# A third place for turned rows, and two small subtractions moved ahead of a larger one, in an fp32-accurate attention and expert kernel

## What is computed

```python
q = (hidden_states @ Wq.T).reshape(B, L, H, D)
k = (hidden_states @ Wk.T).reshape(B, L, KVH, D)
v = (hidden_states @ Wv.T).reshape(B, L, KVH, D)
q = _apply_rope(q, cos, sin)          # the "turned" rows
k = _apply_rope(k, cos, sin)
dt = softplus(hidden_states @ Win.T + dt_bias); g = dt * -exp(A_log_bias)
G = cumsum(g) within a chunk of 128 tokens
scores  = q_chunk @ k_chunk.T ; decay = causal exp(G_i - G_j)
y_intra = (scores * decay) @ (v * dt)
cstates = (k * exp(Glast - G)).T @ (v * dt)      # state handed to the next chunk
y_inter = (q * exp(G)) @ previous state
y = rmsnorm(y_intra + y_inter) * gnorm_w * silu(hidden_states @ Wg.T)
out = y @ Wo.T
```

## Time and profile before

| what | value |
|---|---|
| time, median of 3 runs | 2247.51 us (2245.24 to 2248.74) |
| the profiled execution: its span | 2250.0 us |
| PE busy | 2100.6 us, 93% of the span |
| DVE busy | 1834.7 us, 82% |
| ACT busy | 1402.0 us, 62% |
| POOL busy | 1040.2 us, 46% |
| chain that ended last | 77% PE, 6% DVE, 6% issue, 4% POOL |

### The profile page before, as it was taken

One profiled execution on the slowest core, in us unless ns is written; L12 is line 12 of the kernel. 1 busy time (PEld: TensorE's weight loads), 2 busy tenths in 40 slices (PEclk: granted clock), 3 DMA queues, 4 the chain that ended last, 5 costly groups with the idle time before them and its releaser, 6 DMA issues.

```text
span 2250.0 us, 34037 instructions
## 1 busy us (share of the span) xinstructions
PE 2100.6 (93%) x9568; PEld 1630.9 (72%) x9568; DVE 1834.7 (82%) x3440; ACT 1402.0 (62%) x2732; POOL 1040.2 (46%) x828
## 2 busy tenths in 40 slices
PE   5899999999999999998999999999999999999993
PEld 3677777777777777776677777777777777767772
DVE  5888888888888888868888888888888888737886
ACT  5566666666666666653566666666666666626782
POOL 1344444445454544434364545454545454534661
PEclk8899999999999999999899999999999999979996
DMA  7212121212121212135121212121212121217668
GB/s 255 79 46 58 46 56 47 56 47 56 44 58 38 64 37 66 35 87 173 38 66 38 67 36 62 35 63 38 66 38 66 38 66 38 76 61 255 217 215 315
DMA packets 147547, 182.31 MB, mean 81 GB/s; under 512 B 12935, under 2 KB 89319, under 8 KB 147454
## 3 DMA queue, kind: packets, MB, share of 16 engines
q1 hardware_dynamic: 137310, 155.52, 24.3%
q0 software_dynamic: 8704, 25.21, 3.1%
q10 hardware_dynamic: 1440, 0.58, 0.1%
HBM read 152.90 MB, written 28.37 MB: 81 GB/s over the span
## 4 chain that ended last, share of the span: by engine, by line
PE 77%; DVE 6%; issue 6%; POOL 4%; ACT 3%; DMA 2%; SPq 1%; DVEq 0%; POOLq 0%; ACTq 0%
PE PJ L1242 11%; PE PJ L1244 10%; PE PJ L1243 10%; PE OU L1242 5%; PE OU L1244 5%; PE OU L1243 5%; PE TR L1392 5%; PE YE L1244 2%; PE YE L1243 2%; PE YE L1242 2%; PE SC L1242 2%; PE CS L1242 2%; PE YI L1242 2%; PE CS L1244 2%; PE CS L1243 2%
## 5 line engine op out<-in xcount | busy, mean ns | idle before, releaser
L457 POOL TENSOR_TENSOR zl<-yb,zh 128x512 fp32r<-128x512 f32 x122 | 162.9, 1335 | 318.9 <-ACT zh L972 318.8
L1242 PE MATMUL OU<-woh,zh 128*128 128x512 f32 x488 | 230.4, 472 | 17.7 <-POOL wol L708 10.2
L1765 DVE TENSOR_TENSOR t<-PJ,cosb 128x512 f32<-128x512 f32 x160 | 110.3, 689 | 156.6 <-PE PJ L1244 110.7
L1242 PE MATMUL PJ<-xnh,wqh 128*128 128x512 f32 x544 | 225.4, 414 | 7.9 <-DVE t L1767 7.4
L988 ACT ACTIVATE qh<-t 128x512 fp32r<-128x512 f32 x128 | 80.9, 632 | 218.6 <-DVE t L1770 218.6
L1243 PE MATMUL PJ<-xnl,wqh 128*128 128x512 f32 x544 | 213.9, 393 | 0.0
L1244 PE MATMUL PJ<-xnh,wql 128*128 128x512 f32 x544 | 213.6, 393 | 0.0
L1242 PE MATMUL PJ<-xnh,wgh 128*128 128x512 f32 x512 | 209.1, 408 | 2.9 <-POOL wgl L708 2.9
L1243 PE MATMUL PJ<-xnl,wgh 128*128 128x512 f32 x512 | 204.7, 400 | 0.0
L738 POOL TENSOR_TENSOR gm<-gbc,amask 128x512 f32<-128x512 f32 x128 | 166.9, 1304 | 81.6 <-DMA gbc<-decay_exponents 48.3
L1244 PE MATMUL PJ<-xnh,wgl 128*128 128x512 f32 x512 | 204.4, 399 | 0.0
(11 more groups left out here) (547 smaller groups left out, 6381.7 us busy)
## 6 DMA issues: line engine op xcount, KB each, us to landing
gbc<-decay_exponents SPq DMA_DIRECT2D x128, 256.0 KB, 4.9
stage<-in_wq SPq DMA_DIRECT2D x72, 256.0 KB
stage<-in_wg SPq DMA_DIRECT2D x64, 256.0 KB
stage<-in_wo SPq DMA_DIRECT2D x64, 256.0 KB
gbc<-in_wm SPq DMA_DIRECT2D x48, 256.0 KB
stage<-in_wkv SPq DMA_DIRECT2D x34, 256.0 KB
experts<-in_wm SPq DMA_DIRECT2D x16, 512.0 KB, 5.9
experts<-expert_rows SPq DMA_DIRECT2D x16, 512.0 KB, 13.9
```

The costliest lines, as they stand in the source:

```text
L457: nc.gpsimd.tensor_tensor(lo[:], yb[:, c, :], hi[:].bitcast(F32), ALU.subtract).then_inc(S["zlo"], 1)
L1242: nc.tensor.matmul(out_, a_hi, b_hi, start=first, stop=False)
```

## The change

The turned rows get a table of places, `rope_at`: tile 0 in the first half of `t2`, tile 1 in the second, tile 2 in `y2`, tile 3 in the first half, tile 4 in the second. The waits follow from it: tile 2 waits for the transposes of the raw values, tile 3 for the low part and the transposes of tile 0, tile 4 for the low part of tile 1 (before: of tile 2). On DVE the two subtractions `knlo` and `q3lo` stand ahead of `vw_lo(0)`, and `knlo` ahead of `q3lo`. No computing instruction is added or removed.

```diff
+        rope_at = [t2[:, 0, :], t2[:, 1, :], y2[:], t2[:, 0, :], t2[:, 1, :]]
...
                     def rope_lo(i, hi, lo):
                         at.wait("ropehi", i + 1)
-                        g.tensor_tensor(lo, t2[:, (5 * b + i) % 2, :], hi.bitcast(F32),
+                        g.tensor_tensor(lo, rope_at[i], hi.bitcast(F32),
...
-                            a.activation(hi, t2[:, (5 * b + i) % 2, :], ACT.Copy).then_inc(S["ropehi"], 1)
+                            a.activation(hi, rope_at[i], ACT.Copy).then_inc(S["ropehi"], 1)
...
                         def rope(i, bank):
 
-                            slot = (5 * b + i) % 2
+                            turned = rope_at[i]
                             at.wait("proj", (1, 3, 4, 5, 6)[i])
                             if i == 0:
                                 at.before("ropelo", 4)
                             elif i == 1:
                                 at.before("q3lo", 1)
+                            elif i == 2:
+                                at.wait("tr", 1)
+                            elif i == 3:
+                                at.wait("ropelo", 1)
+                                at.wait("tr", 2)
                             else:
-                                at.wait("ropelo", i - 1)
-                            if i == 2:
-                                at.wait("tr", 2)
+                                at.wait("ropelo", 2)
...
-                        vw_lo(0)
-
-                        at.wait("ropehi", 5)
-                        v.tensor_tensor(ql[:, 3, :], t2[:, (5 * b + 4) % 2, :], qh[:, 3, :].bitcast(F32),
-                                        ALU.subtract).then_inc(S["q3lo"], 1)
                         at.wait("knhi", 1)
                         v.tensor_tensor(knl[:], TR[:, 0:3 * P].rearrange("p (a b) -> p a b", a=3),
                                         knh[:].bitcast(F32), ALU.subtract).then_inc(S["knlo"], 1)
+                        at.wait("ropehi", 5)
+                        v.tensor_tensor(ql[:, 3, :], rope_at[4], qh[:, 3, :].bitcast(F32),
+                                        ALU.subtract).then_inc(S["q3lo"], 1)
+                        vw_lo(0)
```

More of the change, by code:

```diff
@@ L1419, in step @@
                         for i in range(3):
-                            ins = nc.tensor.transpose(TR[:, i * P:(i + 1) * P], t2[:, (5 * b) % 2, i * P:(i + 1) * P],
+                            ins = nc.tensor.transpose(TR[:, i * P:(i + 1) * P], rope_at[0][:, i * P:(i + 1) * P],
                                                       ident[:])
@@ L1765, in rope @@
                             v.tensor_tensor(t1[:], PJ[bank][:], cosb[:], ALU.mult)
-                            v.tensor_tensor(t2[0:hd, slot, :], PJ[bank][hd:D, :], sinb[0:hd, :], ALU.mult)
-                            v.tensor_tensor(t2[hd:D, slot, :], PJ[bank][0:hd, :], sinb[hd:D, :],
+                            v.tensor_tensor(turned[0:hd, :], PJ[bank][hd:D, :], sinb[0:hd, :], ALU.mult)
+                            v.tensor_tensor(turned[hd:D, :], PJ[bank][0:hd, :], sinb[hd:D, :],
                                             ALU.mult).then_inc(S["roperd"], 1)
                             at.wait("roperd", i + 1)
-                            v.tensor_tensor(t2[:, slot, :], t1[:], t2[:, slot, :], ALU.add).then_inc(S["rope"], 1)
+                            v.tensor_tensor(turned, t1[:], turned, ALU.add).then_inc(S["rope"], 1)
                         def weigh(c):
```

## The result

| | before | changed kernel |
|---|---|---|
| median of 6 runs each, us | 2245.15 (2236.71 to 2248.74) | **2226.81** (2212.69 to 2230.52) |
| ratio, 95% interval | | 0.9912 (0.9886 to 0.9939) |
| profiled execution, us | 2250.0 (span) | 2222.85, span 2221.1 |

What follows compares the result with a forecast made beforehand. PE was taken to bound the kernel, starting the scores late by at most 36.9 us in all. Gains of 0.88 us per step, 15 x (0.88 + 0.88) = 26.4, took the median from 2247.5 to 2221.5, range 2213 to 2236.

Steps and rivals of the forecast that it cites:

- The chain and the cause of the idle before the fifth tile: Fifth tile's sum, vwlo, q3lo, then scores; DVE idles 1.19 us before that tile, waiting for its place in `t2`.
- No effect: Rival: the idle before the fifth tile has another cause than the place, so time stays 2247.5; chance 0.05.
- The sum: DVE's sum of the fifth turned tile, b = 0: ends at 884.15 instead of 885.36, behind POOL's second `ql`.
- The held low part: DVE's `q3lo` before the scores, b = 0: behind POOL's `gm` it ends at 885.86, against 885.53 undisturbed.
- the middle of the three prices: `q3lo` with b = 0 ends at 885.53 undisturbed, 885.86 behind `gm`, or 886.05 behind a fully held `gm`; 885.86 taken.
- The new wait before `CS`: PE waits for DVE's `vwl` before the `chunk_state(0)` product, 0.2 to 0.4 us.
- The full hold of the shared data path: DVE's sum delays POOL's `gm` by its whole length; lower bound, gains 0.69 (b = 0) and 0.70 (b = 1), 20.9 us in all.
- PE's idle before the scores: PE's total wait before the scores' product falls from 31.9 to about 5 us, left only with b = 0.
- Each part alone gives little: Old place with new order leaves `chunk_state(0)` at 887.9 as now; the gain is the place's, the order lets it through.
- Given back at intra(0): Rival: `wfl` or pieces ahead meet POOL longer, PE loses up to 0.57 per step; gain 8 to 20; chance 0.13.
- Slower: the clock: Rival: denser PE gets less clock in the loops; 1.5% less cancels the gain, 3% gives 2274; chance 0.04.
- Sum: 15 x (0.88 + 0.88) = 26.4 us: Gain of 0.88 us per step for b = 0 and for b = 1, 15 times each; bounds 20.9 and 31.5.

Runs made afterwards that it cites:

- `gm_held_shift8`: Changed kernel with 8 instructions without effect on DVE ahead of the second half, and POOL's `gm` held until `vwlo` is made: 2210.83 us, ratio 0.9857.
- `before_shift2`: Kernel before the change with two instructions without effect on DVE ahead of the second half: 2250.96 us, ratio 1.0036.
- `before_shift8`: Kernel before the change with eight instructions without effect on DVE ahead of the second half: 2239.53 us, ratio 0.9986.
- `first_shift41`: Changed kernel with 41 instructions of long-met waits on DVE ahead of the first half's loop: 2222.34 us in one run, beside a before of 2245.67.
- `place_only`: Changed kernel with the third place kept but the old order (`vw_lo(0)`, then `ql`, then `knl`): 2242.28 us, ratio 0.9991.

## Why the prediction was right, and which step failed

- **The chain and the cause of the idle before the fifth tile: right.** The wait for POOL's `ql` is gone, and the tile follows the fourth at once. "No effect" fell with it.
- **The sum:** forecast to end 1.21 us earlier and 0.6 behind POOL's `ql`; against the gate projection it ends 1.27 earlier, and 0.55 behind.
- **`gm`:** forecast 1.31 + 0.45 = 1.76, measured 1.74. The held low part, and with it the middle of the three prices: forecast scores 0.5 late, measured 0.46 (871.30 against 870.84). `gm_held_shift8` shows this directly.
- **The new wait before `CS`:** forecast 0.2 to 0.4; `CS` comes 1.00 behind the scores' start where the earlier trace rows have 0.78, about 0.2.
- **The gain per two steps:** forecast 1.76, measured 1.69 in the first half. The full hold of the shared data path, the lower bound of 1.39, is too low here.
- **PE's idle before the scores:** forecast about 5 us, measured 8.0; without the one wait of 4.1 us at step 16, where DVE still does the routing's work, it is 3.9.
- **"Each part alone gives little":** right for the order (it lost 0.19 per two steps, forecast 0). The place alone gave 0.40 of 1.69; the prediction had given the place the whole gain and had left out what keeps it small when the order is old: the pieces of `vwl` meet `gm` and last 1.04 us longer.
- **"Given back at intra(0)"** didn't happen: the 0.89 us of b = 0 is whole at `YI`. **"Slower: the clock"** didn't either: 1.00 in both stretches.

**The step that failed** is "Sum: 15 x (0.88 + 0.88) = 26.4 us": it takes the second half to be like the first. The earlier trace rows are all of the first half, where I looked at one pair of steps. The second half gave 0.40 per step and the turn between the halves 1.1 us where about 2.5 was due, and the loops together about 18 us. The first of these is shown: two more DVE instructions in each loop moved a border of DVE's code from behind the first product of the first tile to ahead of it; with the code shifted by eight the second half gains as the first does. I had called the added wait free by asking what it waits for; it was its place in the instruction list that cost. The turn was not tested, and its cause stays open. PE's wait before the scores of step 16 grew there from 1.5 to 4.1 us, but it is 3.1 us in `before_shift2` and `before_shift8` too, which lack the change, and 1.3 in `first_shift41`, which has it; and steps 14 to 18 last 296.3 us in the kernel before, 292.7 and 294.9 in those two. So one profile of each can't tell 1.1 us of gain there from 2.5.

In numbers, the gain of 19.8 us (at most 25.6) misses the 26.4 and lies just under the prediction's own lower bound of 20.9; it falls into the range from 2213 to 2236 because that was wide enough for gains down to 11.5. The forecast's last step is also off by itself: 2247.5 - 26.4 is 2221.1, not 2221.5. That the median came out 5.3 us from the forecast (5.7 by the sum) is helped by the median of the kernel before, which with six runs is 2.4 us lower than the one the forecast started from.

## What to carry to other kernels

Check a per-step gain in every loop that the program has, not only in one: two loops written from the same code can stand differently in an engine's instruction memory. Where VectorE stands idle for about 2 us at a loop's head and again a few instructions on, released by nothing but "issue", count its instructions: here every loop (of 279 to 284 instructions) that touched three blocks of 128 ran without these stalls, and every one that touched four had them, so a few instructions of padding ahead of the loop, or fewer waits in it, are worth a try. When two engines share a path, what a freed instruction meets next decides; moving a piece with one operand in PSUM into that place made the larger part of this gain (1.29 of 1.69 us per two steps).

## What the runs showed of the hardware

- **VectorE's code loading.** A border every 128 instructions, as far as the transfers tell (8.1 KB each, 122 to 127 instructions apart in the changed kernel's second loop); the stall at 962 in two kernels, at 450 (within one of the count) for the shifted first half; 30 transfers more over the second half's loop when it touches four blocks; 1.6 to 1.9 us idle at the head in the lines shown, and about 2 us ahead of the next border's instruction where no other wait covers it, each round. The Trainium skill, Runtime: NRT & Kernel Launch, section "Instruction fetch mechanics", says that a taken branch out of the window of loaded code forces a fetch; the trace agrees, with a transfer and the idle at the head in each round of a loop that touches four blocks (64 transfers) and neither where it touches three (34). It gives blocks of 256 instructions; here the measurement decides, and the transfers are of 128.
- **VectorE beside POOL.** Four pieces of 128x128 that read two operands from SBUF (where the tiles lie) took 2.17 us beside `gm` in `place_only`, 1.13 without it, all of the loss in the first piece: not only the subtractions and sums collide. POOL's `gm` lost 0.43 us (1.74 for 1.31 in the earlier trace rows) to DVE's sum of 0.73 us in the changed kernel.
